# Three items of the background scatter per pass of the first attention's loop in place of two, and half as many in the stages after it

## The chip, the cores and the metric

One core of a Trainium2 chip runs the whole program in one launch. The metric is the device time of an execution in microseconds (us); the middle of several executions is compared. In what follows PE is TensorE, DVE is VectorE, ACT is ScalarE, POOL is GpSimd and SP is SyncE, which only issues transfers. L2019 means line 2019 of the kernel before.

## What is computed

A graph network of four blocks runs over 3125 nodes (256 values each) and 53125 edges. Each block is a layer norm, a graph layer and a residual sum, then a layer norm, a feed-forward layer and a residual sum. The stages that matter here are the second graph layer (attention with edge features, called the first attention below), the feed-forward layer with 32 experts behind it, and the third graph layer, which needs one small row (20 values) per edge in the order of the edges' source node.

```python
# second graph layer: attention with edge features
k_j = k[src] + e                      # e = edge_attr_256 @ We
v_j = v[src] + e
alpha = jnp.sum(q[dst] * k_j, axis=-1) / jnp.sqrt(32.)
alpha = softmax over the edges of one dst
out = jax.ops.segment_sum(v_j * alpha[:, :, None], dst, n) + x @ Ws + bs
# its feed-forward layer: each node goes through one expert of 32
idx = jnp.argmax(xf @ router_w.T + router_b, axis=-1)
out = relu(relu(xf @ W1[idx] + b1[idx]) @ W2[idx] + b2[idx])
# third graph layer: sums by source node
filt = silu(edge_attr_20 @ Wf1 + bf1) @ Wf2 + bf2
agg = jax.ops.segment_sum(x[dst] * filt, src, n)
```

## The kernel before

**Layout.** The edges are padded to 416 tiles of 128 edges (26 chunks of 16 tiles). Two copies of the edge rows are made in HBM: `by_dst`, sorted by target node, for the first attention, and `by_src`, sorted by source node, for the third graph layer (`filter_stage`). Both are made by the class `RowScatter`: an item is 8 tiles, so there are 52 items for each copy. One item is loaded (`load`), joined with its two key columns by copies on POOL (`join`), and sent by eight indirect DMAs, each of which puts 128 rows where `place` says (`scatter`, L1450, and in the loop `scatter_in_loop`, L1479). The Q7 cores of POOL make the descriptors of each such DMA. They are in the background: the stages that carry them do other work on the other engines. A ring of buffers holds the items. Loading item j + ring waits until item j has landed.

**Stages.** Stages run one after another. Each ends in a barrier of all engines, and with it clears its semaphores, so a stage lasts until its slowest engine is done. A stage gets its share of the items by `src_rows.share(count)`: the merge behind the first attention (`m1`), the norms `n3` and `n4`, and the expert stage `f1` between them.

**The first attention's loop** (`attend1_stage`, stage `a1`) runs over 104 quarters of 4 tiles, 8 quarters to a pass of the hardware loop (`BODY`), 13 passes (`BODIES`). In each quarter POOL waits for `indexed` and `msg_ready` of DVE, issues four gathers of rows of `kv_table` (L2019), then its share of the scatters (`SCATTERED`), with an item's four small copies ahead of its first scatter (L1471 to L1474). PE turns and projects the edge rows, spreads the queries and sums the messages; DVE adds the projected rows to the gathered ones (L2189), multiplies, reduces, and makes the masks (L2197, L2201); ACT copies out of PSUM and stores. DVE reads the index for the quarter three ahead. POOL may run up to three quarters ahead of DVE. ACT loads the next item into the buffer of item k at the start of the quarter that `LOADED` names (`load_in_loop`), and waits there until the eight scatters of item k have landed:

```python
for n in range(SCATTERED[b], SCATTERED[b + 1]):
    k, t = n // 8, n % 8
    if t == 0:
        src_rows.join_in_loop(pool, i, k)
    src_rows.scatter_in_loop(pool, k, t)
```

**The expert stage** (`l1_ffn_stage`, `f1`). POOL first scatters `AHEAD` = 4 items while PE and DVE find each node's expert. Then it waits for `placed` and sends the nodes' rows, sorted by expert, with 25 indirect DMAs (L810). After them come the other items of its share, and last 25 gathers that fetch the experts' results (L819), which DVE adds to the residual (L979). POOL executes in order, so the fetches stand behind all items of the share. PE, ACT and DVE work off the sorted rows meanwhile; SP loads them, stores the results (L792) and loads the items (L1421).

**The norms and the merge.** In `norm_stage` POOL has nothing but its items; in `merge_stage` they stand behind 50 gathers. In both SP loads the items ahead (`share.load`).

## Time and profile before

| | us |
|---|---|
| median of 3 runs | 4857.91 (4852.75 to 4869.78) |
| the profiled execution | 4873.99 |
| its span, first to last instruction | 4872.2 |
| first attention's loop, first gather to last scatter on POOL | 997.3 to 1882.7 |
| m1 | 1944 to 2043 |
| n3 | 2049 to 2079 |
| f1 | 2082 to 2403 |
| n4 | 2406 to 2430 |

Over the span PE is busy 76%, DVE 60%, ACT 34% and POOL 53%. These shares are means over stages with different limits, and say little of a change that moves work from one stage to others. The views by stage do: busy time in one stretch, the waits of one engine in it, and the order of instructions at a stage's end. A bracket in a timeline row is the idle time of the engine ahead of the instruction and what ended it; "issue" there means that the engine waited for nothing that the profile shows.

### The profile page before, as it was taken

To read this page: it belongs to the slowest core of one execution; us is meant where nothing else is said; L and a number is where in the kernel's file an instruction comes from. 1 tells how busy PE (TensorE), PEld (TensorE's weight loads), DVE (VectorE), ACT (ScalarE), POOL (GpSimd) and SP (SyncE) were. 2 spreads that over 40 slices of the span, in tenths; PEclk is the share of its full clock that TensorE was granted. 3 is DMA by queue.
4 is the path that set the end of the run, shared out by engine and by line. 5 is a ranking of instruction groups with operands and counts; after the bars stand their busy time and mean duration, and the time that the engine had idled before them with its cause. 6 is when DMAs were issued, how large, how long until landed. Compare 5 with 4: busy or idle time off the path is not lost. (4 is left out here: it accounts for less than half of the span.)

```text
span 4872.2 us, 75057 instructions
## 1 busy us (share of the span) xinstructions
PE 3686.5 (76%) x20734; PEld 2955.3 (61%) x20786; DVE 2915.4 (60%) x5941; ACT 1667.2 (34%) x3757; POOL 2586.5 (53%) x2597
## 2 busy tenths in 40 slices
PE   7786489869999997135089999279999577777188
PEld 6664367758777785133078888257777466665165
DVE  7788374558988896521278888333333645554653
ACT  5563222013333332001066666133333223333032
POOL 0075767667777773675677777500000277775400
PEclk9986689989999998556599999689999878887579
DMA  5065456489999996333278887310000167666300
GB/s 78 1 211 174 144 186 198 167 267 329 333 330 329 332 336 189 100 88 111 64 198 237 233 229 227 107 62 1 0 0 0 51 179 200 197 197 179 95 14 26
DMA packets 642022, 779.41 MB, mean 160 GB/s; under 512 B 149190, under 2 KB 562361, under 8 KB 638106
## 3 DMA queue, kind: packets, MB, share of 16 engines
q0 software_dynamic: 120624, 316.61, 21.2%
q1 hardware_dynamic: 350852, 284.27, 20.7%
q10 hardware_dynamic: 170374, 176.38, 11.7%
q8 instruction: 90, 1.47, 0.1%
q14 instruction: 82, 0.67, 0.0%
HBM read 509.08 MB, written 272.20 MB: 160 GB/s over the span
## 5 line engine op out<-in xcount | busy, mean ns | idle before, releaser
L2606 POOL DMA_INDIRECT fl_far<-x_table,fl_index x416 | 481.7, 1158 | 144.1 <-issue 126.4
L2340 POOL DMA_INDIRECT a_far<-src_table,a_index x416 | 450.7, 1083 | 132.1 <-issue 124.0
L1450 POOL DMA_INDIRECT by_dst<-dst_row,place x416 | 414.7, 997 | 191.4 <-issue 102.4
L2019 POOL DMA_INDIRECT a_far<-kv_table,a_index x416 | 434.8, 1045 | 145.5 <-issue 113.1
L2643 PE MATMUL ps<-fl_w,fl_hid 128*128 128x256 f32 x1664 | 405.0, 387 | 38.8 <-ACT ps L2715 37.3
L3311 POOL DMA_INDIRECT starts<-p_near,p_at x25 | 24.4, 975 | 708.2 <-DMA starts<-p_zero 693.1
L2053 PE MATMUL ps<-a_w,a_edge_t 128*128 128x256 f32 x1664 | 395.3, 381 | 0.0
L2643 PEld LDWEIGHTS ps<-fl_w,fl_hid 128*128 128x128 f32 x1664 | 312.4, 192 | 88.8 <-issue 48.9
L2053 PEld LDWEIGHTS ps<-a_w,a_edge_t 128*128 128x128 f32 x1664 | 301.1, 191 | 32.6
L1078 ACT ACTIVATE f_hid<-ps,f_bn 128x320 f32<-128x320 f32 x320 | 197.6, 617 | 327.7 <-PE ps L1032 327.7
L1119 DVE SCALAR_TENSOR_TENSOR x_sb<-ps,f_cw,x_sb 128x256 f32 x200 | 96.8, 484 | 343.9 <-PE ps L1043 343.9
L2394 PE MATMUL ps<-a_msg,a_same 128*128 128x264 f32 x832 | 284.0, 493 | 20.1 <-ACT a_msg L2423 17.2
L2189 DVE TENSOR_TENSOR a_far<-ps,a_far 128x1024 f32<-128x1024 f32 x208 | 253.7, 1220 | 68.4 <-PE ps L2053 63.6
L1479 POOL DMA_INDIRECT by_src<-a_src_row,a_src_row_place_now x208 | 219.1, 1053 | 79.7 <-issue 48.6
L2154 ACT COPY a_out<-ps 128x528 f32<-128x528 f32 x208 | 125.2, 602 | 387.9 <-PE ps L2101 387.5
L1450 POOL DMA_INDIRECT by_src<-src_row,place x208 | 206.3, 992 | 79.5 <-issue 59.7
L2064 PE MATMUL ps<-xn_sb,a_spread 128*128 128x256 f32 x832 | 222.1, 389 | 31.6 <-issue 30.1
L2101 PE MATMUL ps<-a_msg,a_same 128*128 128x264 f32 x832 | 232.0, 403 | 12.5 <-ACT a_msg L2143 8.5
L2433 ACT COPY a_out<-ps 128x528 f32<-128x528 f32 x208 | 125.0, 601 | 306.9 <-PE ps L2394 306.9
L2394 PEld LDWEIGHTS ps<-a_msg,a_same 128*128 128x128 f32 x832 | 189.4, 242 | 61.2 <-issue 21.6
L230 PE MATMUL ps<-const_sb,xn_sb 128*128 128x128 f32 x300 | 49.9, 338 | 228.9 <-DVE xn_sb L219 228.9
L2064 PEld LDWEIGHTS ps<-xn_sb,a_spread 128*128 128x128 f32 x832 | 150.3, 190 | 76.6 <-issue 56.2
(536 smaller groups left out, 9338.9 us busy)
## 6 DMA issues: line engine op xcount, KB each, us to landing
partial<-a_out ACTq DMA_DIRECT2D x208, 546.0 KB, 4.4
a_edge<-by_dst SPq DMA_DIRECT2D x104, 516.0 KB
partial_f<-fl_out ACTq DMA_DIRECT2D x26, 2056.0 KB, 10.2
dst_row<-in_edge_attr SPq DMA_DIRECT2D x52, 1024.0 KB, 6.1
xn_sb<-q_table SPq DMA_DIRECT2D x416, 128.0 KB
fl_keys<-key_rows SPq DMA_DIRECT2D x26, 1024.0 KB, 5.3
a_keys<-local_rows SPq DMA_DIRECT2D x104, 128.0 KB
xt<-partial SPq DMA_DIRECT2D x14, 512.0 KB, 4.8
```

Of the source, the lines that this page charges most:

```text
L1078: nc.scalar.activation(hid[:, e % 2, layer, m, half * HALF:(half + 1) * HALF], ps[:, n % 4, 0:HALF], ACT.Relu, bias=bn[:, layer, 2, e * KD ...
L1450: self.nc.gpsimd.indirect_dma_start(out=self.table, out_offset=bass.IndirectOffsetOnAxis(ap=self.place[:, n:n + 1], axis=0), in_=self.row[ ...
L1479: self.nc.gpsimd.indirect_dma_start(out=self.table, out_offset=bass.IndirectOffsetOnAxis(ap=self.place_now[:, k, t:t + 1], axis=0), in_=se ...
L2019: gathered[b % 4].count(nc.gpsimd.indirect_dma_start(out=far[:, b, u, :], out_offset=None, in_=kv_table, in_offset=bass.IndirectOffsetOnAx ...
L2053: last = nc.tensor.matmul(ps[:, PROJ[v], t * D:(t + 1) * D], edge_t[:, v, t, k, :], w_sb[:, k, :], start=(k == 0), stop=(k == KD - 1))
L2064: last = nc.tensor.matmul(ps[:, NEAR[v], t * D:(t + 1) * D], spread[:, b % 2, v * 2 + t, :], near[:, b % 4, v * 2 + t, :], start=True, sto ...
L2101: last = nc.tensor.matmul(ps[:, 6 + t, 0:SEG], same[:, s, v * 2 + t, :], msg[:, s % 2, v * 2 + t, :], start=True, stop=True)
L2189: nc.vector.tensor_tensor(kv, e, kv, ALU.add).then_inc(added, 1)
L2340: gathered[b].count(nc.gpsimd.indirect_dma_start(out=far[:, b, u, :], out_offset=None, in_=src_table, in_offset=bass.IndirectOffsetOnAxis( ...
L2394: last = nc.tensor.matmul(ps[:, SUMS[v] + t, 0:SEG], same[:, s, v * 2 + t, :], msg[:, s % 2, v * 2 + t, :], start=True, stop=True)
L2606: gathered[q * 4 + t // 4].count(nc.gpsimd.indirect_dma_start(out=far[:, q, t, :], out_offset=None, in_=table, in_offset=bass.IndirectOffs ...
L2643: last = nc.tensor.matmul(ps[:, FILT[v], u % 2 * D:(u % 2 + 1) * D], hid[:, qb % 2, k, u * P:(u + 1) * P], w2_sb[:, k, :], start=False, st ...
```

## The change

The ring of the scatters by source has three buffers in place of two. In the first attention's loop a pass carries three items in place of two: three scatters behind the gathers of each quarter in place of two. Items 0 and 1 of a pass are the halves of chunk i as before, and item 2 is the first half of chunk 25 - i, counted from the far end (the branches `k == 2` in `RowScatter` were there). ACT loads the next items at quarters 2, 5 and 7 of a pass in place of 3 and 7. So 39 of the 52 items are sent in the loop in place of 26. The shares behind it fall from 2, 2, 20 and 2 items (m1, n3, f1, n4) to 1, 1, 10 and 1.

```diff
@@ attend1_stage
-    A_BODY, SCATTERED, LOADED = 2, (0, 2, 4, 6, 8, 10, 12, 14, 16), {3: 0, 7: 1}
+    A_BODY, SCATTERED, LOADED = 3, (0, 3, 6, 9, 12, 15, 18, 21, 24), {2: 0, 5: 1, 7: 2}
@@ gnn_ffn_kernel
-        src_rows = RowScatter(core, ctx, "src", 2, by_src, a["edge_attr_20"], keys_f[:, ::-1], place[:, 1])
+        src_rows = RowScatter(core, ctx, "src", 3, by_src, a["edge_attr_20"], keys_f[:, ::-1], place[:, 1])
...
-            merge_stage(core, "m1", 0, base, count, partial, carry, SEG, HEADS, inv, share=src_rows.share(2))
+            merge_stage(core, "m1", 0, base, count, partial, carry, SEG, HEADS, inv, share=src_rows.share(1))
...
-                    norm_stage(core, "n3", xt, src_rows.share(2), early)
+                    norm_stage(core, "n3", xt, src_rows.share(1), early)
...
-                    l1_ffn_stage(core, xt, early, src_rows.share(20), by_expert, from_expert)
+                    l1_ffn_stage(core, xt, early, src_rows.share(10), by_expert, from_expert)
...
-                norm_stage(core, "n4", None, src_rows.share(2), table=x_table)
+                norm_stage(core, "n4", None, src_rows.share(1), table=x_table)
```

POOL, first attention's loop, the first two quarters of a pass, before (`a_far` are the gathered rows, `a_src_row` the item's buffer):

```order
L2019 DMA a_far<-kv_table,a_index 128x512 x4
...
L1471 COPY a_src_row<-a_src_row_taken 128x8x20
...
L1479 DMA by_src<-a_src_row,a_src_row_place_now 53248x22 x2
L2014 REGISTER_ALU
L2019 DMA a_far<-kv_table,a_index 128x512 x4
L1479 DMA by_src<-a_src_row,a_src_row_place_now 53248x22 x2
```

The same place now, with the third quarter, in which the second item's copies stand:

```order
L2019 DMA a_far<-kv_table,a_index 128x512 x4
...
L1471 COPY a_src_row<-a_src_row_taken 128x8x20
...
L1479 DMA by_src<-a_src_row,a_src_row_place_now 53248x22 x3
L2014 REGISTER_ALU
L2019 DMA a_far<-kv_table,a_index 128x512 x4
L1479 DMA by_src<-a_src_row,a_src_row_place_now 53248x22 x3
L2014 REGISTER_ALU
L2019 DMA a_far<-kv_table,a_index 128x512 x4
L1479 DMA by_src<-a_src_row,a_src_row_place_now 53248x22 x2
L1471 COPY a_src_row<-a_src_row_taken 128x8x20
```

One more scatter stands ahead of each quarter's gathers, and three groups of copies in a pass.

POOL, expert stage, from the sends of the sorted rows to the fetches, now (before, ten more groups of two copies and eight scatters stand in the run):

```order
L810 DMA partial<-xn_sb,f_spot_i 7168x256 x25
L1450 DMA by_src<-src_row,place 53248x22 x4
L1433 COPY src_row<-src_row_taken 128x8x20
L1434 COPY src_row<-keys_f 128x8x2
L1450 DMA by_src<-src_row,place 53248x22 x8
...
L1450 DMA by_src<-src_row,place 53248x22 x4
L819 DMA xn_sb<-partial_f,f_spot_i 128x256 x25
```

The fetches stand behind 6 items in place of 16.

## Rows read from the trace of the kernel before

**Rows 1.** Two passes: length; busy PE, PEld, DVE, ACT, POOL; clock; DMA; GB/s.

```profile
1133.20:1201.70 68.50, 65.81 (x328) 54.52 (x327) 61.76 (x89) 23.71 (x69) 52.61 (x57) 1.00 1.03 332
...
1747.20:1815.10 67.90, 65.41 (x328) 54.64 (x327) 61.27 (x89) 23.49 (x68) 52.01 (x56) 1.00 1.07 333
```

**Rows 2.** Waits of POOL, 1000 to 1882 us (total us, times, longest).

```profile
POOL a_far L2019 <- issue: 112.8, 370, 0.3
```

**Rows 3.** Groups of instructions, 990 to 1960 us (xcount | busy, mean ns | idle).

```profile
L2019 POOL DMA_INDIRECT a_far<-kv_table,a_index x416 | 434.8, 1045 | 145.5 <-issue 113.1 <-DVE a_index L2181 32.4
...
L1479 POOL DMA_INDIRECT by_src<-a_src_row,a_src_row_place_now x208 | 219.1, 1053 | 79.7 <-issue 48.6 <-POOL a_src_row_place_now L1474 24.0 <-DVE a_index L2181 6.4
```

**Rows 4.** Timeline of POOL in the loop, around an item's copies (start, us).

```profile
1411.52 1.06 POOL L2019 DMA_INDIRECT a_far<-kv_table,a_index  x1 [0.30 <-issue]
1412.58 0.65 POOL L1471 COPY a_src_row<-a_src_row_taken 128x160 f32<-128x160 f32 x1
...
1414.55 1.05 POOL L1479 DMA_INDIRECT by_src<-a_src_row,a_src_row_place_now  x1 [0.92 <-POOL a_src_row_place_now L1474]
```

**Rows 5.** Tile `by_src`: the loop's scatters, ns min/median/max.

```profile
L1479 POOL DMA_INDIRECT by_src<-a_src_row,a_src_row_place_now x208: 992/1029/1519, 1003.9 to 1881.7; - x104
```

**Rows 6.** Timeline of all engines in the loop: one stretched gather.

```profile
1421.16 0.69 DVE L2201 TENSOR_TENSOR a_same<-a_keys,local_rank_b 128x512 f32<-128x512 bf16 x1
1421.20 1.52 POOL L2019 DMA_INDIRECT a_far<-kv_table,a_index  x1 [0.30 <-issue]
```

**Rows 7.** Timeline of all engines: an item's last scatter, ACT's load behind it.

```profile
1406.23 1.00 POOL L1479 DMA_INDIRECT by_src<-a_src_row,a_src_row_place_now  x1 [0.31 <-issue]
...
1412.96 0.37 ACTq L1458 DMA_DIRECT2D a_src_row_taken<-in_edge_attr  x1
```

**Rows 8.** Timeline of all engines: the loop's last gather, the last quarter's first add.

```profile
1879.02 1.00 POOL L2019 DMA_INDIRECT a_far<-kv_table,a_index  x1 [0.31 <-issue]
...
1892.37 1.22 DVE L2189 TENSOR_TENSOR a_far<-ps,a_far 128x1024 f32<-128x1024 f32 x1
```

**Rows 9.** Timeline of all engines at the end of m1.

```profile
2029.52 1.16 POOL L1450 DMA_INDIRECT by_src<-src_row,place  x1 [0.30 <-issue]
...
2031.85 11.54 SPq L1421 DMA_DIRECT2D src_row_taken<-in_edge_attr  x2
...
2032.80 1.49 DVE L3027 TENSOR_TENSOR x_sb<-x_sb,m_own 128x1280 f32<-128x1280 f32 x1
```

**Rows 10.** Timeline of all engines at the end of n3.

```profile
2061.85 8.03 ACT L241 COPY xt<-ps 128x256 f32<-128x256 f32 x23
...
2067.43 13.40 SPq L1421 DMA_DIRECT2D src_row_taken<-in_edge_attr  x2
...
2078.34 0.97 POOL L1450 DMA_INDIRECT by_src<-src_row,place  x1 [0.30 <-issue]
```

**Rows 11.** Timeline of all engines in f1, where the experts' work ends.

```profile
2264.60 0.37 SPq L792 DMA_DIRECT2D partial_f<-xt  x1
...
2275.42 0.34 POOL L1433 COPY src_row<-src_row_taken 128x160 f32<-128x160 f32 x1
...
2285.95 0.34 POOL L1433 COPY src_row<-src_row_taken 128x160 f32<-128x160 f32 x1
```

**Rows 12.** The page's DMA issues: out<-in, KB each, us to landing.

```profile
partial_f<-xt SPq DMA_DIRECT2D x14, 512.0 KB, 3.2
```

**Rows 13.** Timeline of all engines in f1, where the fetches begin.

```profile
2366.90 1.04 POOL L819 DMA_INDIRECT xn_sb<-partial_f,f_spot_i  x1 [0.31 <-issue]
...
2374.98 1.49 DVE L979 TENSOR_TENSOR x_sb<-x_sb,xn_sb 128x1280 f32<-128x1280 f32 x1 [110.40 <-DMA xn_sb<-partial_f,f_spot_i]
```

**Rows 14.** Timeline of all engines at the end of n4.

```profile
2418.45 6.82 SPq L197 DMA_DIRECT2D x_table<-xn_sb  x5
...
2426.04 0.97 POOL L1450 DMA_INDIRECT by_src<-src_row,place  x1 [0.30 <-issue]
```

**Rows 15.** Stretch of the last attention's loop, columns as in Rows 1.

```profile
4250.00:4350.00 100.00, 80.36 (x361) 65.94 (x359) 50.80 (x123) 32.47 (x115) 78.37 (x72) 0.78 0.68 192
```

## The prediction

> **What bounds the kernel now.** I read the stretches first, since the change only moves work of one engine, POOL, from four short stages into one long loop. What counts is who sets the pace in the loop, and who ends last in each of the four.
>
> In the loop two passes show the same picture [rows 1]: 68.5 and 67.9 us for eight quarters, PE busy 65.8 and 65.4 of them, DVE 61.8 and 61.3, POOL 52.6 and 52.0, the DMA engines at a share of 1.03 to 1.07. By these shares PE looks like the bound and POOL seems to have a quarter of its time free. It has none. Its waits in the loop are all "issue", 0.3 us each: 370 of them ahead of gathers, 112.8 us in sum [rows 2]. The reader is to see that this is the fixed step from one indirect DMA to the next, not spare time, and that no wait for DVE's index or messages of any length stands in the list. A pass of POOL adds up from its parts: 32 gathers at 1.045 us and 16 scatters at 1.053 [rows 3] make 50.3, their 48 steps of 0.305 make 14.6, and an item's copies take 1414.55 - 1412.58 = 1.97 from the end of the gather to the next scatter, 1.665 over a usual step, twice 3.3 [rows 4]. The sum is 68.2, which is the pass. So POOL issues without a pause from the first gather to the last scatter, 885.4 us, and PE, nearly full too, keeps up with it. The loop is balanced between the two, and has no room on POOL.
>
> Behind the loop the stages are read from their ends. In m1 DVE is done at 2034.3, but SP's second load of an item waits for scatters to land and ends at 2043.4 [rows 9]. In n3 ACT ends at 2069.9, POOL's last scatter at 2079.3 and SP's second load at 2080.8 [rows 10]. In f1 the experts' last result is out at 2264.6 [rows 11], but the fetches begin at 2366.9, right behind the last scatter, and DVE sits idle 110.4 us for them [rows 13]. In n4 POOL ends at 2427.0, SP's last store of the table goes out at 2425.3 and has yet to land before the stage can end [rows 14].
>
> **The loop: what is added.** 104 scatters move in. Each takes 1.053 + 0.305 = 1.358 us, together 141.2. Thirteen more groups of copies at 1.665 are 21.6. So POOL needs 162.8 us more, 12.5 a pass, and a pass takes 80.7 to 81.0. Nothing hides it: PE's work of 65.8 and DVE's of 61.8 a pass lie beside it and are shorter, so these two now wait for POOL, and the 162.8 are on the path. Queued behind each added scatter are the next quarter's gathers, for which DVE's add waits.
>
> What POOL cannot pass on is its lead. Now the last gather ends at 1880.02 and the add of that quarter starts at 1892.37, 12.35 later [rows 8]. With POOL the bound the others follow as close as they may. How close, ACT decides: it waits at the start of a quarter for the item's scatters to land, and the load goes out 1412.96 - 1407.23 = 5.7 us after the last scatter's end [rows 7]. In the last quarter of a pass that scatter is now the third behind the gathers, 3 x 1.36 = 4.1, so the lag is about 9.8 there. That gives back 2.5, up to 5 if a less busy queue lands sooner. The lag is no cost by itself, since POOL is allowed almost three quarters of 10.1 us ahead. SP's one more load at the start costs under 0.5. I take 162.8 - 3 = 160.
>
> The size of a scatter is the least certain term. Their median is 1.029, the least 0.992, the most 1.519 [rows 5]; the long ones stand beside DVE's mask, as the gather of 1.52 us that starts 0.04 after L2201 [rows 6]. The mask comes once a quarter, before and after. With no stretched DMA at all the 624 old ones would save 624 x (1.048 - 1.02) = 17; with one in each quarter, 0.5 us each, 104 x 0.5 - 17 = 35 more is lost. The phase of the two engines decides, and I take the present mean, since L2201 lasts 0.69 of a step of 1.35, so that half of random starts fall in it, about as now. This is 143 to 195 around 160, with the ends unlikely.
>
> The Trainium skill has a rule for it (SBUF — State Buffer, Who interferes with whom): a DVE instruction with two inputs in SBUF, as L2201, and a POOL instruction block each other on a shared port, and the order of issue decides who loses. The rows agree, and by that rule the whole range from none to one in each quarter is open, which is the range worked out above.
>
> **The stages behind it: what is removed.** One item in a quiet stage takes 2285.95 - 2275.42 = 10.5 us [rows 11].
>
> m1 sends one item less. POOL is then done at 2030.7, where the first item's eighth scatter ends, SP's last load follows within 2 (2043.4 against POOL's 2041.9 now), and DVE's 2034.3 is last [rows 9]. It gains 2043.4 - 2034.3 = 9.1, not 10.5.
>
> n3 sends one item less, and with three buffers its copies find the item already loaded. POOL and SP's second load drop out; ACT's 2069.9 is last, or SP's first load at 2067.8 [rows 10]. It gains 2080.8 - 2069.9 = 10.9; the experts' weights, 4 MB issued at the stage's start, may not have landed then, so I take 10.
>
> f1 has 10 items. The first four are ahead of `placed` as before, so nothing changes up to the sends. Six are left where 16 were: 6 x 10.5 from 2161.8, and some waits for their loads, end near 2242, before the experts do. What is late next is the last store: out at 2264.6, landed 3.2 later [rows 12]. Fetches start at 2268 in place of 2366.9, 98.7 earlier. The 25 fetches and DVE's last add behind them remain. It is 99 and not 10 x 10.5 = 105, because the experts' own end comes into sight.
>
> n4 sends one item less, which POOL did beside the table's stores. These still end the stage: nothing [rows 14].
>
> Removed together: 9.1 + 10 + 98.7 = 118. Thirteen items cost 12.3 each in the loop, and give back 9.1 each behind it: dearer in the loop by copies of 1.665 in place of some 0.3 and by DVE's stretches, and partly in places where they had been hidden.
>
> **The sum.** 160 - 118 = +42 us. The profiled execution, 4873.99 with a span of 4872.2, would become 4916. It lies 16 over the median of the runs, 4857.91, so the median becomes 4900, 0.9% more.
>
> **Rivals.** (1) The other side: POOL's pace in the loop gives way. The loop's DMA engines are at a share of 1.03 and PE at 96% [rows 1], so POOL's long instructions could be their doing, and a looser loop would let them shrink. The floor is the quiet pace: 416 gathers at 1.00 [rows 8] + 0.305 and 312 scatters at 1.275 (an item's 10.5 less its copies, by eight) make 543 + 398, and 39 groups of copies at 1.5 make 58, in all 999. Against 885.4 that is +114; with -3 and -118 the result is -7, 4851. It decides from the point at which the mean of gathers and scatters falls under 1.01 us. Against it: the minimum of 0.992 and the median of 1.029 in a full loop show that most are at their floor already. By a rule of the Trainium skill (DMA: Bandwidth & Descriptors, Issuing engines are not separate DMA queues), an issuing engine's time is usually small beside the transfers on the shared DMA engines; the added scatters, a few bytes each, would be free in the loop and the sum would be -118. The list of waits [rows 2] speaks against it: a POOL held up by transfers would show longer steps than 0.3.
>
> (2) PE's clock falls. In the loop it is 1.00 (2.4 GHz) in both passes. With 15 us of each pass idle it may drop to 1.2 GHz at times, as in the last attention's loop, where POOL also sets the pace and the granted clock is 0.78 [rows 15]. At 0.78 PE's 65.8 become 84.4 a pass, 3.6 over POOL's 80.8, 13 times 47: 4947. At 0.82 or more it costs nothing. PE is fuller here than there, so I put it between, 4925. The Trainium skill (TensorE: Matmul & The Clock Gate, What's actually happening) says that the throttled state is the default and activity releases it, which would make PE recover whenever it becomes the bound; no row yet shows this loop with gaps.
>
> (3) The short stages don't gain: n3 or m1 end on a transfer that I don't see. +19: 4919.
>
> That the change does not do what it says I give nothing: the order of the instructions shows the three scatters and the shorter runs.
>
> **Chances.** The forecast 0.77, its own range 4884 to 4920 from the size of a scatter. Rival 1: 0.06, of which 0.02 below. Rival 2: 0.12. Rival 3: 0.05. The range that should hold 8 in 10 leaves out rival 1, the upper half of rival 2 and the unlikely ends of the stretches: 4876 to 4930. About 0.3%, 14.6 us, is what a measurement of this kernel can tell from no change. Faster by more: 0.02. Within it, 4843 to 4872: 0.07. Slower: 0.91.
>
> **What would show it.** In the profile after: the loop from first gather to last scatter near 1048 us in place of 885; POOL's waits in it still 0.3 alone; PE busy near 66 of 81 a pass; a granted clock at or near 1.00. In m1 and n3 DVE and ACT last. In f1 the fetches 2 to 4 us behind the last store, and DVE's wait ahead of its first add near 12 in place of 110. I am wrong if POOL shows waits of more than 1 us in the loop (then another engine sets the pace), if its mean scatter is far from 1.05, or if a stage behind the loop ends as late as before.

## The result, and the profile after

The changed kernel takes 4890.74 us in the median of ten runs (4867.65 to 4904.14), the kernel before 4856.92 beside it (4841.82 to 4874.20). The ratio is 1.006, with a 95% interval of 1.0039 to 1.008: slower, by 0.6%. The profiled execution took 4890.67, its span is 4888.9. Ratios here are those of the measurement and not quotients of the two medians beside them, from which they differ by up to 0.2%. The medians lie 33.8 us apart and the two profiled executions 16.7, because the profiled execution of the kernel before, 4873.99, lay 17 above its median and the changed kernel's at it.

Where the 16.7 us between the two spans come from, by the starts and ends that the traces give (us):

| part of the program | before | after | change | forecast |
|---|---|---|---|---|
| up to the loop's first gather | 997.3 | 993.3 | -4.0 | 0 |
| first gather to last scatter | 885.4 | 1036.1 | +150.7 | +162.8 |
| last scatter to the start of m1 | 61.6 | 55.4 | -6.2 | -3 |
| m1 | 104.6 | 92.2 | -12.4 | -9.1 |
| n3 | 33.3 | 21.2 | -12.1 | -10 |
| f1 | 323.4 | 230.8 | -92.6 | -98.7 |
| n4, and `filter_stage` up to its loop | 38.3 | 35.9 | -2.4 | 0 |
| `filter_stage`'s loop | 608.9 | 596.9 | -12.0 | 0 |
| last attention's loop | 577.9 | 585.4 | +7.5 | 0 |

The rest is +0.2. The last two loops are counted from 0.8 us ahead of their first gather, where POOL's first instruction of the loop stands, to the end of the last gather. The loop and its end gave +144.5 for 160, the stages behind it -119.5 for 118.

The rows that answer to those of before follow. Two passes of the loop in the stretches view (length; busy PE, PEld, DVE, ACT, POOL with their counts; clock; DMA; GB/s), the answer to [rows 1]:

```profile
1152.20:1231.00 78.80, 68.57 (x326) 56.34 (x326) 61.48 (x88) 23.38 (x68) 59.91 (x69) 0.94 0.96 292
1639.00:1718.00 79.00, 68.07 (x327) 55.84 (x326) 61.22 (x88) 22.91 (x68) 60.10 (x69) 0.93 0.97 287
```

A pass is 79 us in place of 68. POOL is busy 60 of them and PE 68, so by shares alone PE would be the bound again. The waits of POOL from 1000 to 2030 us, the answer to [rows 2], say that it is not:

```profile
POOL a_far L2019 <- issue: 127.5, 397, 1.9
POOL by_src L1479 <- issue: 81.9, 268, 0.3
POOL by_src L1479 <- POOL a_src_row_place_now L1474: 31.8, 35, 0.9
POOL a_far L2019 <- DVE a_index L2181: 4.6, 15, 0.3
```

The steps of 0.3 us and POOL's waits for its own copies fill the list. Beside them stand four single steps of 1.9 us, 240 us apart, 6.5 us over the usual step in all, of which nothing in the trace shows the cause. The prediction had named waits of more than 1 us as a sign of being wrong; these are four in 727 steps, and none is put down to another engine for more than 0.9. POOL waits for nobody, and PE has 10 us of a pass to spare. The groups of POOL's instructions in the whole loop (count, busy us, mean ns, idle before), the answer to [rows 3]:

```profile
L2019 POOL DMA_INDIRECT a_far<-kv_table,a_index x416 | 434.0, 1043 | 151.8 <-issue 128.4 <-DVE a_index L2181 23.4
L1479 POOL DMA_INDIRECT by_src<-a_src_row,a_src_row_place_now x312 | 320.6, 1027 | 118.7 <-issue 81.9 <-POOL a_src_row_place_now L1474 31.8 <-DVE a_msg L2218 2.6
L1471 POOL COPY a_src_row<-a_src_row_taken 128x160 f32<-128x160 f32 x39 | 13.5, 346 | 0.2
```

Two timelines. First POOL around an item's copies, the answer to [rows 4]; the copies end within 0.75 us, and the wait of 0.88 behind them is the larger half of what they cost:

```profile
1415.21 1.03 POOL L1479 DMA_INDIRECT by_src<-a_src_row,a_src_row_place_now  x1 [0.30 <-issue]
1416.55 1.00 POOL L1479 DMA_INDIRECT by_src<-a_src_row,a_src_row_place_now  x1 [0.31 <-issue]
1417.52 0.36 POOL L1471 COPY a_src_row<-a_src_row_taken 128x160 f32<-128x160 f32 x1
...
1419.13 0.99 POOL L1479 DMA_INDIRECT by_src<-a_src_row,a_src_row_place_now  x1 [0.88 <-DVE a_msg L2218]
```

Then all engines at the loop's end, the answer to [rows 7, 8]:

```profile
2024.40 1.00 POOL L2019 DMA_INDIRECT a_far<-kv_table,a_index  x1 [0.31 <-issue]
...
2028.42 0.97 POOL L1479 DMA_INDIRECT by_src<-a_src_row,a_src_row_place_now  x1 [0.30 <-issue]
2029.21 1.23 DVE L2189 TENSOR_TENSOR a_far<-ps,a_far 128x1024 f32<-128x1024 f32 x1 [1.97 <-DMA a_far<-kv_table,a_index]
2031.25 0.36 ACTq L1458 DMA_DIRECT2D a_src_row_taken<-in_edge_attr  x1
2031.65 0.22 ACT L2143 COPY a_msg<-a_weight 128x32 f32<-128x32 f32 x1 [6.31 <-DMA by_src<-a_src_row,a_src_row_place_now]
...
2036.41 1.22 DVE L2189 TENSOR_TENSOR a_far<-ps,a_far 128x1024 f32<-128x1024 f32 x1 [4.25 <-PE ps L2053]
```

The quarter's first add starts 3.8 us behind the last gather's end (12.35 before), since the gathers themselves release it. The second comes 7.2 later, because ACT stood 6.31 us at the quarter's start for the third scatter to land, and PE's next projection hangs on ACT's copy.

The ends of m1 and n3, the answer to [rows 9, 10]: DVE's last sum in m1, then the start of n3; ACT's last copies in n3, then the start of f1.

```profile
2171.82 0.33 SPq L1421 DMA_DIRECT2D src_row_taken<-in_edge_attr  x1
2172.74 1.49 DVE L3027 TENSOR_TENSOR x_sb<-x_sb,m_own 128x1280 f32<-128x1280 f32 x1
...
2177.01 3.37 DVE L210 BATCH_NORM_STATS2 n_stats<-x_sb 128x6 f32<-128x256 f32 x10 [2.78 <-PEq L148]
...
2187.01 0.97 POOL L1450 DMA_INDIRECT by_src<-src_row,place  x1 [0.30 <-issue]
...
2189.12 8.09 ACT L241 COPY xt<-ps 128x256 f32<-128x256 f32 x25 [1.58 <-PE ps L230]
...
2198.22 0.23 DVE L910 CAST f_lt<-const_sb 128x128 bf16<-128x128 f32 x1 [2.13 <-PEq L148]
```

A timeline does not show what POOL does last in a stage: its sequencer stands in a `DRAIN` that ends some us behind its last indirect DMA, and the barrier can't come before that. This has to be asked for by the line of the stage's end. Its rows for the end of m1 (ns, start), before and after, and for the end of f1 after:

```profile
L2874 POOLq DRAIN  x1: 11432/11432/11432, 2035.9 to 2035.9; - x1
```

```profile
L2874 POOLq DRAIN  x1: 13655/13655/13655, 2161.8 to 2161.8; - x1
```

```profile
L764 POOLq DRAIN  x1: 22179/22179/22179, 2404.6 to 2404.6; - x1
```

In m1 it ends at 2047.33 before, 5.5 us behind POOL's last scatter and 3.9 behind SP's last load, and at 2175.44 after, 4.8 behind the last scatter and 1.2 behind the end of DVE's last sum. The barrier follows within 0.04 us both times. So POOL is last in m1 in both kernels. In n3 it was last before (2081.18), and ACT is after (its copies end at 2197.21).

And the fetches in f1, the answer to [rows 13]. They wait for the last store to land, issued at 2380.27 + 3.31, and DVE's wait ahead of its first add is 12.32 us where it was 110.40:

```profile
2380.27 3.31 SPq L792 DMA_DIRECT2D partial_f<-xt  x2
...
2387.40 1.04 POOL L819 DMA_INDIRECT xn_sb<-partial_f,f_spot_i  x1 [23.54 <-DMA partial_f<-xt]
...
2395.50 1.49 DVE L979 TENSOR_TENSOR x_sb<-x_sb,xn_sb 128x1280 f32<-128x1280 f32 x1 [12.32 <-DMA xn_sb<-partial_f,f_spot_i]
```

### The profile page after: what moved, and what is told of

Read it like the earlier page. It is cut to its first block and busy times, and to the rows that moved or that the text cites. A ratio compares the mean times of both kernels' runs of the same rounds, so it can differ in the third digit from the quotient of the medians.

```text
span 4888.9 us, 75299 instructions
## 1 busy us (share of the span) xinstructions
PE 3717.1 (76%) x20786; PEld 2970.8 (61%) x20786; DVE 2913.0 (60%) x5941; ACT 1659.1 (34%) x3757; POOL 2579.0 (53%) x2623
## 5 line engine op out<-in xcount | busy, mean ns | idle before, releaser
L2606 POOL DMA_INDIRECT fl_far<-x_table,fl_index x416 | 469.7, 1129 | 152.3 <-issue 126.4
L2340 POOL DMA_INDIRECT a_far<-src_table,a_index x416 | 458.2, 1102 | 132.3 <-issue 124.3
L2019 POOL DMA_INDIRECT a_far<-kv_table,a_index x416 | 434.0, 1043 | 151.8 <-issue 128.4
L2053 PE MATMUL ps<-a_w,a_edge_t 128*128 128x256 f32 x1664 | 406.6, 389 | 0.0
L1479 POOL DMA_INDIRECT by_src<-a_src_row,a_src_row_place_now x312 | 320.6, 1027 | 118.7 <-issue 81.9
L2189 DVE TENSOR_TENSOR a_far<-ps,a_far 128x1024 f32<-128x1024 f32 x208 | 253.9, 1220 | 213.8 <-PE ps L2053 148.3
L2101 PE MATMUL ps<-a_msg,a_same 128*128 128x264 f32 x832 | 246.9, 423 | 116.0 <-ACT a_msg L2143 101.6
L2053 PEld LDWEIGHTS ps<-a_w,a_edge_t 128*128 128x128 f32 x1664 | 311.1, 197 | 36.0
L2394 PE MATMUL ps<-a_msg,a_same 128*128 128x264 f32 x832 | 285.7, 495 | 16.6 <-ACT a_msg L2423 13.4
L2101 PEld LDWEIGHTS ps<-a_msg,a_same 128*128 128x128 f32 x832 | 165.8, 206 | 157.3 <-issue 114.4
L2064 PE MATMUL ps<-xn_sb,a_spread 128*128 128x256 f32 x832 | 222.5, 390 | 36.4 <-issue 35.6
L2394 PEld LDWEIGHTS ps<-a_msg,a_same 128*128 128x128 f32 x832 | 190.8, 244 | 57.5 <-issue 17.9
L2379 PE MATMUL ps<-a_first,a_same 128*128 (+1 forms) x832 | 134.0, 288 | 87.3 <-DVE a_same L2462 87.3
```

The source lines that it names most:

```text
L1479: self.nc.gpsimd.indirect_dma_start(out=self.table, out_offset=bass.IndirectOffsetOnAxis(ap=self.place_now[:, k, t:t + 1], axis=0), in_=se ...
L2019: gathered[b % 4].count(nc.gpsimd.indirect_dma_start(out=far[:, b, u, :], out_offset=None, in_=kv_table, in_offset=bass.IndirectOffsetOnAx ...
L2053: last = nc.tensor.matmul(ps[:, PROJ[v], t * D:(t + 1) * D], edge_t[:, v, t, k, :], w_sb[:, k, :], start=(k == 0), stop=(k == KD - 1))
L2064: last = nc.tensor.matmul(ps[:, NEAR[v], t * D:(t + 1) * D], spread[:, b % 2, v * 2 + t, :], near[:, b % 4, v * 2 + t, :], start=True, sto ...
L2101: last = nc.tensor.matmul(ps[:, 6 + t, 0:SEG], same[:, s, v * 2 + t, :], msg[:, s % 2, v * 2 + t, :], start=True, stop=True)
L2189: nc.vector.tensor_tensor(kv, e, kv, ALU.add).then_inc(added, 1)
```

## The experiments

**Two kinds of chips.** The experiments fell on four chips, of two kinds. On two of them the kernel before takes 4840 to 4847 us, as in the recorded pair (4857); on the other two it takes 6017 to 6019. Kernels are compared within a kind only. Lengths of stages and loops come from one profile of each kernel, and those of the kernel before and the changed one from the recorded pair. The second kind has a part of its own below; the first kind decides on the forecast, which was made for it.

| kernel, on chips of the first kind | ratio to the kernel before, 95% interval | loop | m1 to n4 |
|---|---|---|---|
| before (profiled) | 1 | 885.4 | 499.6 |
| changed | 1.006, 1.0039 to 1.008 | 1036.1 | 380.1 |
| changed, copies first | 0.9975, 0.9964 to 0.9987 | 995.4 | 379.4 |
| changed, copies first, loads later | 0.9999, 0.9939 to 1.0058 | 1002.2 | 378.8 |
| changed, third item left out | 0.9962, 0.9927 to 0.9997 | 936.3 | 378.3 |
| before, copies first | 0.9985, 0.9952 to 1.0019 | 876.2 | 500.5 |
| before, second item left out | 1.016, 1.012 to 1.020 | 909.4 | 502.2 |

The loop is counted from its first gather to POOL's last indirect DMA, m1 to n4 up to `filter_stage`'s loop, as in the first table. The two kernels with an item left out carry the filling with zeros ahead of the loop, 11 to 19 us, as the first gather comes so much later.

### Copies ahead of the gathers: is POOL's own time the currency?

```diff
@@ attend1_stage, POOL
                         m = i * BODY + b
+                        for n in range(SCATTERED[b], SCATTERED[b + 1]):
+                            if n % 8 == 0:
+                                src_rows.join_in_loop(pool, i, n // 8)
                         pool.wait_ge(indexed, m + 1)
...
                             if t == 0:
-                                src_rows.join_in_loop(pool, i, k)
+                                src_rows.joined_in_loop(pool, i, k)
```

`joined_in_loop` holds the wait for the four copies, `join_in_loop` the copies alone.

> The changed kernel, with one move: an item's four copies stand ahead of the quarter's four gathers on POOL, the wait for them stays ahead of the item's first scatter, so it finds them long done. Nothing is left out. In the changed kernel that wait takes 0.92 us, 39 times, and the wait for the fourth copy hides nothing else. Theory (POOL's own time sets the pace of the loop): about 0.6 to 0.9 us a group go, 39 groups, 23 to 36 us; the loop from first gather to last scatter falls from 1036 to 1000 to 1013 and the time from 1.006 of the kernel before to 0.999 to 1.001. Rival A (the loop is paced by something else by now, PE's clock or transfers): within 5 us of the changed kernel. Rival B (copies that stand closer to DVE's instructions are stretched by them): the copies' mean rises over 0.5 us and eats the gain. The four runs before this one came from a chip on which this program takes 6019 us in place of 4857, with a loop paced by pauses of PE that wait for nothing in the profile, and POOL waiting 3 to 4 us a quarter for DVE's index; on such a chip this edit gives nothing by either theory, since POOL has time there.

Measured: 4834.66 us against 4847.11, 0.9975. The loop is 995.4 us long, 40.7 shorter than the changed kernel's, a little over the 36 that the theory allowed; rival A (within 5 us) is out. POOL around the copies:

```profile
1397.01 0.97 POOL L1482 DMA_INDIRECT by_src<-a_src_row,a_src_row_place_now  x1 [0.30 <-issue]
1397.97 0.45 POOL L1471 COPY a_src_row<-a_src_row_taken 128x160 f32<-128x160 f32 x1
1398.38 0.32 POOL L1473 COPY a_src_row<-keys_f 128x8 f32 x2
1398.63 0.18 POOL L1474 COPY a_src_row_place_now<-place 128x8 int32 x1
1398.97 1.06 POOL L2025 DMA_INDIRECT a_far<-kv_table,a_index  x1 [0.16 <-POOL a_src_row_place_now L1474]
```

From the end of one indirect DMA to the start of the next there are 0.99 us across the copies, where the changed kernel has 1419.13 - 1417.55 = 1.58 at the place shown above. Over the whole loop the gaps with copies in them sum to 65.2 us for 39 in the changed kernel and to 37.8 for 38 here, so 27 of the 41 us are these. The others are shorter indirect DMAs, 1038 ns for 1043 and 1011 for 1027 in the mean (7 us), and the changed kernel's four steps of 1.9 us (6 us), which this one doesn't have. Every microsecond that POOL was given came out as time: at three items it is POOL that bounds this loop. Rival B is out too, the large copy's mean is 358 ns.

### The same with two items

The same edit to the kernel before.

> The kernel before, with an item's copies ahead of the quarter's gathers, as in the changed kernel with copies first, where that took 41 us off the loop of 39 groups (1.04 each). Nothing is left out. Here are 26 groups, so POOL needs 27 us less. Theory (balance of POOL and PE at two items): PE's floor of 66 to 67 a pass lets at most half of it through, the time falls by 5 to 20 us, ratio 0.996 to 0.999. Rival A (POOL alone bounds the kernel before): 25 to 28 us, ratio 0.9945. Rival B (PE bounds it): nothing, within 3 us.

Measured: 4838.67 against 4839.89, ratio 0.9985 with an interval from 0.9952 to 1.0019, and a loop of 876.2 for 885.4. The theory's lower end: of 24 us of gaps that went, 9 came out. The groups and the waits of POOL in this loop show where the rest went:

```profile
L2025 POOL DMA_INDIRECT a_far<-kv_table,a_index x416 | 442.7, 1064 | 146.6 <-issue 116.8 <-DVE a_index L2187 29.3 <-POOL a_src_row_place_now L1474 0.5
```

```profile
POOL a_far L2025 <- DVE a_index L2187: 21.5, 25, 0.9
```

The gathers are longer by 19 ns in the mean than in [rows 3], 7.9 us in sum. The wait row (1040 to 1900 us) shows POOL waiting 0.9 us for DVE's index about twice a pass, where the list of [rows 2] has steps of 0.3 at most. A stretch of one pass:

```profile
1467.40:1535.04 67.64, 65.48 (x328) 54.63 (x327) 61.08 (x89) 22.84 (x68) 51.83 (x56) 1.00 1.06 335
```

Ten passes from the third on are 67.6 us long to within 0.1. PE works 65.5 of them, as in [rows 1], and no loop in any run is shorter, so I take this for the floor. So "balanced between the two" was right, and it can be given a number: at two items POOL stood 9 us above the floor in the whole loop. In time the edit can't be told from no change.

### One item in a pass

```diff
+                            if k == 1:
+                                if t == 0:
+                                    pool.wait_ge(src_rows.loaded[k], i * 16 + 16)
+                                    pool.sem_inc(src_rows.passed, 1)
+                                    pool.sem_inc(src_rows.joined, 4)
+                                continue
                             if t == 0:
                                 src_rows.join_in_loop(pool, i, k)
```

> The kernel before once more with the loop's second item loaded but neither copied nor scattered (left out; the same filling). It asks what bounds the loop when POOL has 12.5 us a pass less than in the kernel before. Theory (POOL and PE were balanced at two items): PE's 65.5 to 66 a pass takes over, the loop falls from 885 to 855 to 878, and POOL waits several us a quarter for DVE's index or messages. Rival A (POOL alone was the bound, and PE's busy time stretches with it): the loop falls by 100 or more. Rival B (PE was the bound already): 883 or more.

Measured: 909.4 us, longer than with two items. Rival A is out, and so is the theory's size: not 855 to 878 but 909. By its number rival B (883 or more) holds, but PE is not the bound that it names, since PE works 65 to 67 of passes of 70 to 74. Two of its passes, and then the rows on `a_edge` (the edge rows that SP loads: idle time of the engines ahead of its users, in us and times, 1150 to 1850 us), first of this kernel and then of the kernel before:

```profile
1283.66:1357.43 73.77, 65.31 (x324) 54.13 (x323) 61.36 (x89) 22.82 (x69) 41.23 (x44) 1.00 1.00 318
...
1712.15:1782.23 70.08, 67.16 (x327) 55.79 (x327) 61.07 (x89) 22.89 (x69) 41.22 (x44) 0.98 0.99 316
```

```profile
  DMA a_edge<-by_dst: 85.6, 29
```

```profile
  DMA a_edge<-by_dst: 35.3, 30
```

With POOL ahead of everyone, edge rows come in late, and PE stands ahead of its transposes for ACT's copies. PE's work is about the same, 65.3 and 67.2 us; the passes are 70 to 74 us long. The DMA engines are at a share of 1.00 in all of these loops, and that the gathers, which now go out in bursts as soon as DVE's index allows, are what delays the loads is my reading; no run took it apart. Nor is the item that is loaded and then left alone, which this kernel has and the kernel before has not, excluded as a cause. What stands is that a loop with one item is no shorter than one with two, so the second costs nothing, and the third its full price.

### The third item left out

```diff
+                            if k == 2:
+                                if t == 0:
+                                    pool.wait_ge(src_rows.loaded[k], i * 16 + 16)
+                                    pool.sem_inc(src_rows.passed, 1)
+                                    pool.sem_inc(src_rows.joined, 4)
+                                continue
```

> The changed kernel once more with the loop's third item loaded but neither copied nor scattered (left out; a small stage ahead of the loop fills the table with zeros in its place, which took 24 to 30 us by the first trace and is taken off by hand). On a chip where POOL issues without a pause in this loop. Theory (POOL's own work paces the loop): the loop falls from 1036 to 885 within 8, the four stages behind it last as long as in the changed kernel, so the gain behind the loop stands alone: the time less the filling is 118 to 122 under the kernel before, a ratio near 0.981 with the filling. Rival A (the third load, ACT's wait for it or the ring costs): the loop stays above 900. Rival B (PE's clock cost part of the 150): PE's busy time a pass falls by more than 2 us.

Measured: 4827.21 against 4839.89, 0.9962, and not 0.981. The stages behind the loop last 378.3 us in this run and 380.1 in the changed kernel, against 499.6 and 500.5 in two kernels with the old shares. So the gain behind the loop is 119.5 to 122, whatever the loop does; that part of the forecast (118) stands by itself. The loop, however, took 936.3, so rival A (the third load, ACT's wait for it or the ring) holds by its number: 51 over the 885.4 of two items in the kernel before. PE's busy time in a pass falls by 2.0 us to 66.4, which is the bound of rival B's sign, but PE had 10 us to spare in the changed kernel, so I don't count it as a cost. In it POOL waits up to 7.3 us for the index, and the waits for edge rows are as above (1040 to 1900 us and 1150 to 1850 us):

```profile
POOL a_far L2041 <- DVE a_index L2209: 72.5, 46, 7.3
```

```profile
  DMA a_edge<-by_dst: 108.1, 34
```

The two items stood in the first five quarters here, three scatters to a quarter, with none in the last two. I read the 51 us as the cost of that unevenness, the same as in the run with one item, whose eight scatters fill four quarters. This isn't shown: the run that was to show it, with the scatters spread, fell on the other kind of chip (below), and on this kind rival A stands untested. As a measure of the third item's cost this run is spoilt: it gives 100, a comparison with two even items (the kernel before) gives 151.

### Loads later

```diff
-    A_BODY, SCATTERED, LOADED = 3, (...), {2: 0, 5: 1, 7: 2}
+    A_BODY, SCATTERED, LOADED = 3, (...), {3: 0, 6: 1}
@@ ACT's quarter
+                    if b == 1 and (not isinstance(i, int) or i > 0):
+                        src_rows.load_in_loop(act, i - 1, 2)
```

> The changed kernel with copies first, and ACT's loads of the next items moved to where their scatters have landed (quarters 3 and 6, and quarter 1 of the next pass for item 2). Nothing is left out. Theory (POOL paces, ACT's waits cost nothing but at the end): 0 to 6 us under the kernel with copies first alone (0.9975), from the last quarter's second add. Rival (ACT's waits of 5 to 7 us at a quarter's start hold up PE, and through its clock or DVE's index the rest): 15 us or more, and PE's busy time in a pass changes.

Measured: 0.9999 (0.9939 to 1.0058), four runs that lie 60 us apart, and a loop of 1002.2 for 995.4. ACT's waits for scatters, 141.7 us in 35 waits before the edit, are gone from its list. At the end of the loop the second add follows the first at once, 2.9 us later and not 5.9:

```profile
2002.60 1.23 DVE L2197 TENSOR_TENSOR a_far<-ps,a_far 128x1024 f32<-128x1024 f32 x1 [0.42 <-DMA a_far<-kv_table,a_index]
2005.47 1.22 DVE L2197 TENSOR_TENSOR a_far<-ps,a_far 128x1024 f32<-128x1024 f32 x1
```

That is the 3 us that the theory named, and nothing else came of it; the rival's 15 us did not. ACT's 140 us of waits in the loop cost nothing but at its end. The 7 us by which the loop is longer are longer gathers and scatters (1050 and 1023 ns for 1038 and 1011).

### The other kind of chip

The same code takes 6019 us there. A POOL instruction lasts as long as on the first kind (a gather 1028 ns, a scatter 1008 in the changed kernel with loads later), and so do DVE's and ACT's. What differs is how instructions arrive. SP's register instructions ahead of a quarter's loads (1500 to 1850 us; count, ns min/median/max), first in the kernel before on the first kind, then in the kernel with a ring of three on the second:

```profile
L1996 SPq SEQ_ASSERT  x162: 18/18/18, 1500.0 to 1849.8; - x162
```

```profile
L1996 SPq SEQ_ASSERT  x128: 2/18/709, 1510.7 to 1849.8; - x128
```

An instruction that takes 18 ns each time takes up to 709 there. PE shows the same as waits for nothing ahead of its weight loads on L2064: 82.2 us in 59 waits of up to 4.5 in 800 us, where the kernel before on the first kind has 55.7 in 82 of up to 2.2 in 880; ahead of those on L2101 it is 48.5 us for 4.7. SP, which in the kernel before waits 178.7 us of the loop for PE, waits 30 us for it in these 800. Two-item loops take 1102 to 1123 us, and POOL waits for DVE's index 52 times in these 75 quarters, 193 us in all, so it isn't the bound. It looks like a late supply of instructions; that, and what makes it late, isn't shown.

| kernel, on chips of the second kind | ratio, 95% interval | loop | m1 to n4 |
|---|---|---|---|
| changed, loads later | 1.0038, 1.0017 to 1.006 | 1237.4 | 437.3 |
| changed, third item left out | 0.9866, 0.9832 to 0.990 | 1123.1 | 440.9 |
| changed, third item's copies only | 0.9887, 0.9855 to 0.9919 | 1127.4 | 441.8 |
| changed, third left out, two items even | 0.9859, 0.9828 to 0.9889 | 1102.3 | 440.0 |
| before, second item left out | 0.9905, 0.9878 to 0.9931 | 1032.2 | 556.4 |
| before, ring of three | 1.0003, 0.9986 to 1.002 | 1117.5 | 554.5 |
| changed, copies on ACT | 1.0108, 1.0089 to 1.0128 | 1262.1 | 438.3 |

> The changed kernel, in which the loop's third item is loaded but neither copied nor scattered (that part of the computation is left out; a small stage ahead of the loop fills the table with zeros in its place and costs some 20 to 30 us, to be read from the trace). Behind the loop nothing differs from the changed kernel. Theory (POOL's own work paces the loop): first gather to last scatter falls from 1036 to 885 within 8 us, PE at 1.00 again, and the whole lies 150 under the changed kernel plus the filling: about 4765. Then the loop's cost is 150 and the gain behind it 118 to 120. Rival A (what costs in the loop is the third load and ACT's wait for it, or the ring of three): the loop stays above 950. Rival B (the loop's end and the stages behind are coupled, so part of the 120 behind is lost when the loop is short): m1 to n4 longer than in the changed kernel by more than 5.

> As the kernel with the third item left out, but its copies are made (its scatters alone are left out; the same filling). It splits the 150 us of the loop between 13 groups of copies and 104 scatters. The recorded forecast had 21.6 for the copies (1.665 a group) and 141.2 for the scatters (1.358 each), 163 together, 12 too many. If scatters are full price, copies must have been nearly free: this loop is 8 longer than the one without them. If the scatters were the cheaper ones (1.25 each, since the mean of all gathers and scatters fell a little), this loop is 20 to 22 longer. I expect the second, +20, with the remaining 130 for the scatters.

> The kernel before, in which the loop's second item is loaded but neither copied nor scattered (left out; the same filling ahead of the loop). It asks what bounds the loop when POOL has 12.5 us a pass less. Theory (POOL and PE were balanced at two items): PE's 65.5 to 66 a pass takes over, the pass is 66 to 67.5 in place of 68, and the loop falls from 885 to 855 to 878. POOL then shows waits of several us for DVE's index or messages once a quarter. Rival A (POOL alone was the bound, and PE's busy time stretches with it): the loop falls by 100 or more, towards 725. Rival B (PE was the bound already, POOL's back-to-back issue is chance): the loop stays at 883 or more. By the theory the first item of a pass costs almost nothing in this loop, the second 1 to 2 us, and only the third its full price.

> The changed kernel, with ACT's loads of the next items one quarter later for items 0 and 1 (quarters 3 and 6) and in quarter 1 of the next pass for item 2, where their scatters have landed. Nothing is left out. ACT's 172 us of waiting for scatters go below 60. Theory (POOL is the bound, so ACT's waits cost nothing but at the very end): the loop from first gather to last scatter stays at 1036 within 5, the last quarter's second add comes 3 to 4 us earlier, the time is 0 to 6 us lower than the changed kernel's. Rival (ACT's waits hold up PE and DVE and through them POOL): the loop is 15 us or more shorter.

None of these four can speak on the forecast's loop, since POOL doesn't pace it here. Read by themselves: the gain behind the loop is 556.4 - 437.3 = 119, as on the first kind. The third item costs 1237.4 - 1123.1 = 114, of which its copies are 4 (1127.4 - 1123.1) and its scatters 110; against two even items it is 135. The kernel with all three items has its loads in other quarters than the one with two, so part of the 114 can be theirs; the changed kernel as it stands was not run here. The second item costs 91 (from 1032.2 to 1123.1). I had no theory by which a scatter costs over 1 us in a loop where POOL waits 2 to 3 us a quarter; that is open.

The even spreading has this edit over the kernel with the third item left out:

```diff
-    A_BODY, SCATTERED, LOADED = 3, (0, 3, 6, 9, 12, 15, 18, 21, 24), {2: 0, 5: 1, 7: 2}
+    A_BODY, SCATTERED, LOADED = 3, (0, 2, 4, 6, 8, 10, 12, 14, 24), {3: 0, 7: 1}
```

> The changed kernel with the loop's third item loaded but neither copied nor scattered (left out; the filling with zeros ahead of the loop, 11 to 19 us), and items 0 and 1 spread evenly, two scatters a quarter as in the kernel before. In the run with the third item left out they stood three to a quarter in the first five quarters of a pass and none in the last two, and its loop took 936 us, not 883. Theory (the evenness made that difference, since POOL's pace in the first quarters was over PE's): the loop is 880 to 890, the time is the kernel before less 119 and the filling on top, ratio 0.977 to 0.980, and the third item's whole cost in the loop is 150. Rival (the ring of three or the third load makes the loop longer): 920 or more again.

It gave 1102.3 for 1123.1: the sign that evenness was to have, 21 us of it and not 51, in a loop that POOL doesn't pace. The rival (the ring of three or the third load lengthens the loop) can be set aside for this kind, since this loop, with both, is no longer than the 1117.5 of the kernel with neither the load nor the third buffer in its loop. For the first kind of chip the 51 us stay explained by argument only.

Copies on ACT (`copy_in_loop`, the four copies as ACT's, a quarter behind each load):

> The changed kernel with an item's four copies in the loop made by ACT in place of POOL (a quarter after each load, and the loads where the scatters have landed: quarters 3 and 6, and quarter 1 of the next pass). POOL then issues only gathers and scatters. Nothing is left out. POOL's pass in the kernel with copies first is 76.6 us, of which some 3 x 1.3 are copies and their steps. Theory (POOL's own time paces the loop at three items): the pass falls to 72.5 to 73.5, 56 DMAs at 1.30, the loop to 945 to 960 us, and the time to 0.987 to 0.991 of the kernel before; ACT has 50 us of each pass free and takes 3 to 4 us more without harm. Rival A (at this pace PE with its clock falling in the gaps is the bound): the pass stays above 75. Rival B (ACT's copies, which wait for loads to land, hold up PE's copies of turned edges): the loop is longer than the 995 of the kernel with copies first.

It gave 1262.1 for the 1237.4 of its twin with copies on POOL. POOL has nothing to gain there, and the loop is 25 us longer; whether by ACT's work or by its waits for the loads isn't shown. On the first kind of chip, where the gaps with POOL's copies still sum to 37.8 us, it wasn't measured.

### The ring of three alone

```diff
-        return n % self.RING, n // self.RING + self.rounds
+        return n % self.RING, n // self.RING + (self.rounds if n % self.RING < 2 else 0)
@@ gnn_ffn_kernel
-        src_rows = RowScatter(core, ctx, "src", 2, by_src, ...)
+        src_rows = RowScatter(core, ctx, "src", 3, by_src, ...)
```

> The kernel before, its loop and its shares unchanged, but with three buffers for the stages behind the loop. Nothing is left out. It separates the ring from the items: the recorded forecast gave n3 and m1 a gain by one item less and by loads that are done earlier. Theory (the item itself costs, 10.5 each, and POOL stays last): n3 keeps its 33 us within 3, m1 its 105 within 3 (SP's load is last there with two buffers or three), and of the 110 us of DVE's wait in f1 less than 10 go; the time is within 0.3% of the kernel before. Rival (the wait for loads is what makes an item dear): m1 and n3 lose 5 or more each and f1 20 or more, ratio below 0.995.

Measured: 1.0003 and m1 105.8 us, as expected; but n3 holds a surprise. POOL's second item in n3, in the kernel before and with three buffers:

```profile
2064.02 0.99 POOL L1450 DMA_INDIRECT by_src<-src_row,place  x1 [0.31 <-issue]
2073.74 0.32 POOL L1433 COPY src_row<-src_row_taken 128x160 f32<-128x160 f32 x1 [8.73 <-DMA src_row_taken<-in_edge_attr]
```

```profile
2722.52 0.98 POOL L1450 DMA_INDIRECT by_src<-src_row,place  x1 [0.30 <-issue]
2723.50 0.34 POOL L1433 COPY src_row<-src_row_taken 128x160 f32<-128x160 f32 x1
```

In the kernel before POOL stands 8.73 us for a load (n3 brings 4 MB of weights at the same time); with three buffers it doesn't, and its last scatter ends 21.6 us after n3's start where it was 30.4. n3 then ends with ACT, 30.3 us long, where on this kind of chip it takes 33.9 with the old ring (before, second item left out). POOL's `DRAIN` ends 26.2 us after n3's start, where it was 32.3. ACT's own end is later on this chip; on the first kind ACT ends 21 us after the start, and POOL's `DRAIN` would still be last. So by my estimate about 6 of n3's 12 us would have come from the ring, without moving an item. "POOL stays last" was wrong here. In m1 it was right, but not that SP's load is last there: POOL's `DRAIN` ends at 2705.79, and the barrier follows within 0.04 us.

### What varies without a change

`filter_stage`'s loop is the same in every kernel. Its gathers (count, busy us, mean ns) in the kernel before, the changed one, with copies first at three items and at two, and with loads later:

```profile
L2606 POOL DMA_INDIRECT fl_far<-x_table,fl_index x416 | 481.7, 1158 | 144.1 <-issue 126.4 <-DVEq L2800 17.7
```

```profile
L2606 POOL DMA_INDIRECT fl_far<-x_table,fl_index x416 | 469.7, 1129 | 152.3 <-issue 126.4 <-DVEq L2800 25.9
```

```profile
L2612 POOL DMA_INDIRECT fl_far<-x_table,fl_index x416 | 452.1, 1087 | 158.9 <-issue 127.4 <-DVEq L2806 31.5
```

```profile
L2612 POOL DMA_INDIRECT fl_far<-x_table,fl_index x416 | 441.4, 1061 | 155.4 <-issue 126.5 <-DVEq L2806 28.9
```

```profile
L2614 POOL DMA_INDIRECT fl_far<-x_table,fl_index x416 | 484.7, 1165 | 152.3 <-issue 126.4 <-DVEq L2808 25.9
```

The same code takes 580 to 612 us by how many of its gathers are stretched, and the last attention's loop 574 to 585. So the -12.0 and +7.5 of the first table are no effects of the change, and a single profile of this kernel can't settle less than some 15 us outside the stage that was touched.

## Why the prediction was right

The forecast was 4900, between 4876 and 4930, slower with 0.91; it came out at 4890.74. Where the time goes was right; that the median came within 9 us of the forecast is in part luck, as the last paragraph of this section shows. Point by point:

- **POOL paces the loop.** Right, and shown: its waits in the loop are steps of 0.3, its own copies and four single steps of 1.9, and 27 us less of waits around copies, with 13 of shorter DMAs and other waits, made a loop 41 us shorter. The kernel with two items gave 9 us for the same edit, so the balance of POOL and PE there was seen rightly too.
- **The third item's price, 162.8.** It was 150.7. By its parts in the two traces: gathers 434.8 to 434.0, scatters 219.1 to 320.6, gaps with copies 48.7 to 65.2, steps and other waits 182.8 to 216.3. The scatters were sized at 1.053 each, 109.5 together, and brought 101.5. The reason is in the tile's row, of the changed kernel, beside [rows 5]:

```profile
L1479 POOL DMA_INDIRECT by_src<-a_src_row,a_src_row_place_now x312: 967/998/1509, 999.9 to 2028.4; - x156
```

  The median falls from 1.029 to 0.998. A scatter that follows a gather has a median of 1.03, the next 1.00, a third one 0.97, by their place in the row of equal instructions. I had priced the added scatter by the mean of all, when what the change adds is the one at the row's end, and that is cheaper. The gaps came to 50.0 for the 53.3 forecast (104 steps, 31.7, and 13 groups, 21.6). The copies are 12.5 of them over the usual step, 9 less than forecast: I took 1.665 over the step for a new group from one place, and the groups' mean gap fell from 1.87 to 1.67, as the large copy's mean fell from 505 to 346 ns. The other steps are 37.5 for 31.7, the four of 1.9 us included.
- **The stretches beside L2201** took the middle of their range: 43 DMAs of over 1.2 us stand in the changed loop and 45 in the one before, all beside that instruction, with 104 more to hit. The changed loop's trace tells which DMAs these are: of the 66 that start while L2201 runs 41 take over 1.2 us, up to 1.54; of the 59 that had started before it 2 do, and L2201 keeps its 0.68 us in the median, 0.82 at most. The Trainium skill (SBUF — State Buffer, Who interferes with whom) has a DVE instruction with two inputs in SBUF and a POOL instruction that reads SBUF block each other by the order of issue. The rows agree, also in this: L2189, L2209 and L2218 have one input in PSUM, and of the 345 DMAs that start while one of them runs none takes over 1.05 us. The same section infers that such a DVE instruction leaves POOL's making of descriptors alone; here POOL's indirect DMAs got longer beside it, and the measurement decides.
- **Rival 1 (POOL's pace gives way, 4851)** did not come: the mean of gathers and scatters is 1.036, and it needed 1.01. Its direction was there in part, through the 0.97 of a third scatter. The rule it leaned on in the Trainium skill (DMA: Bandwidth & Descriptors, Issuing engines are not separate DMA queues) does not hold for this loop: what left the other stages, 120 us, came back as 150 of issuing, in a loop whose length followed POOL's own time when the copies moved.
- **Rival 2 (PE's clock)** happened and cost nothing. The granted clock is 0.93 to 0.94 in [rows 1]'s answer: about once a pass it falls to 1.2 GHz for 7 to 10 us; in the six falls looked at PE had stopped 2 to 5 us before, for 6 to 9 us in one piece. PE's busy time rises from 65.6 to 68.4 a pass and stays 10 under POOL's 79. The bound I gave it (no cost from 0.82 up) held.
- **Rival 3 (the short stages don't gain)** did not come: m1 and n3 gained 24.5 together for the 19 forecast.
- **The loop's end** gave 6.2 for 3. The first add came 3.8 behind the last gather, and not 9.8, since ACT's wait stands ahead of the second half of the quarter and not of the first. I had put the wait in the right place and on the wrong add.
- **m1, 12.4 for 9.1.** The step that failed is what ends the stage. I had SP's last load (2043.4) last before and DVE's sum after; POOL's `DRAIN` is last in both. The whole item came out, 11.7 us from m1's start to POOL's last scatter, and 0.7 by a shorter `DRAIN`. **n3, 12.1 for 10**: the 1 us held back for the weights came, but one stage later. PE waits 3.4 us for them at f1's start, and the last store lands 188.2 us after that start where it was 185.4. **f1, 92.6 for 98.7**: the fetches begin 189.2 after its start for 284.7, 95.5 earlier, with the last store last as said. The other 2.9 are lost at its end: DVE is done 225.8 us after the start, 95.5 earlier too, but POOL's `DRAIN` ends 2.5 behind DVE's, where before the two ended within 0.1. **n4, 2.4 for 0**: it ended with POOL's `DRAIN` at 2431.51, 1.1 behind the landing of the last store, and now ends with the store. What the forecast had not priced is the ring's part in n3.
- **Moved together**: 119.5 for 118 behind the loop, the best of the terms, and 121 to 122 again with the third item left out.

So the forecast's net of +42 for the profiled execution was 25 too high: 15.5 in the loop and its end, 1.5 behind it, and 8.5 in parts of the program that vary by themselves. By the medians it was 8 too high, 42 for 33.8. The stages that the change touches sum to 25 in the two profiles; the other 9 us between the medians can't be placed, since the unchanged loops vary by more than that. The mechanism is right by the profiles, and the median is as near as it is with the help of these 9.

## What to carry to other kernels

When an engine issues without a pause, its free share in the profile is not room: count its instructions with the step between them, and expect all that is added there to be paid. Fill a loop up to the point at which its two fullest engines balance, here two items, and before another is added look for waits of the engine on itself: putting four copies ahead of four gathers made the changed kernel faster than the kernel before (0.9975), where moving the items alone had made it slower. With the copies first, two items (0.9985) and three (0.9975) can't be told apart. Price an added instruction by the row of its place in the sequence, and before a stage's end is read from the last DMA or the last sum, look at the `DRAIN` rows of every engine there.

## What the runs showed of the hardware

- An indirect DMA on POOL took less time behind equal ones: medians of 1.03, 1.00 and 0.97 us for the first, second and third scatter behind gathers, and of 1.04, 1.02, 1.00 and 1.00 for the four gathers behind scatters.
- An indirect DMA on POOL that waits for POOL's own copies starts 0.88 to 0.92 us behind the last of them; one that doesn't wait for them starts 0.16 us behind.
- POOL's closing `DRAIN` of a stage ended 1.5 to 7.6 us behind its last indirect DMA in the stages m1 to n4, and was what the barrier waited for in m1 (5.5 us before, 4.8 after) and in f1 after the change (6.0).
- Less work on POOL made the loop longer: 909 us with one item a pass (the second loaded and left alone), 885 with two. Why isn't shown.
- Two of the four chips of the experiments run this program 24% slower, with the instructions of POOL, DVE and ACT as long as on the others and pauses between them.
